# Probabilities times context in three rounded terms for four of twelve tiles

## The reference

```python
kv = context @ Wkv;  k, v = split(kv);  q = layernorm(x) @ Wq
dots = einsum('bhnd,bhmd->bhnm', q, k) * SCALE
dots = dots - (1 - mask)[:, None, :, None] * 1e6
out = einsum('bhnm,bhmd->bhnd', softmax(dots), v)
x = x + out @ Wout + bout
h = gelu(einsum('etd,edf->etf', layernorm(x).reshape(8, 56, 128), w1) + b1)
x = x + einsum('etf,efd->etd', h, w2) + b2
```

## Time and profile before

| what | us |
|---|---|
| median of 3 runs | 395.54 (395.53 to 396.33) |
| the profiled execution's own time | 395.39 |
| its span | 393.7 |
| a batch without a pair (155.94 to 195.70) | 39.76 |
| a batch with a pair (195.70 to 243.00) | 47.30 |
| DVE busy in these two | 30.19 and 36.49 |
| ACT busy in these two | 22.73 and 24.91 |

### The profile page before, as it was taken

The page is one execution under the profiler, slowest core; times in us unless marked ns, Lnnn a source line. Parts: engine busy times, 40 slices in busy tenths (PEclk is TensorE's granted clock), DMA queues, the critical chain, the costliest instruction groups (busy, mean ns, idle before and its releaser), DMA issues.

```text
span 393.7 us, 5563 instructions
## 1 busy us (share of the span) xinstructions
PE 384.8 (98%) x1701; PEld 277.6 (70%) x1701; DVE 282.7 (72%) x469; ACT 205.2 (52%) x273; POOL 63.7 (16%) x68
## 2 busy tenths in 40 slices
PE   7999999999999999999999999999999999999995
PEld 6667667767676777767776877667776776677674
DVE  4887778677867689677867688678867687266443
ACT  3546454565447444675356354575367344755421
POOL 0803401600070002500160003400250000000000
PEclk9999999999999999999999999999999999999999
DMA  7692010350035002142035003151121001200000
GB/s 246 208 273 51 10 69 1 92 144 0 2 83 152 2 1 63 44 149 93 3 91 140 0 0 78 39 169 60 33 73 49 0 0 31 82 2 0 3 2 3
DMA packets 23686, 25.00 MB, mean 64 GB/s; under 512 B 1240, under 2 KB 20600, under 8 KB 23672
## 3 DMA queue, kind: packets, MB, share of 16 engines
q1 hardware_dynamic: 20648, 19.45, 15.9%
q0 software_dynamic: 3024, 5.38, 5.3%
HBM read 24.59 MB, written 0.23 MB: 63 GB/s over the span
## 4 chain that ended last, share of the span: by engine, by line
PE 93%; DVE 4%; ACT 1%; DMA 1%; issue 1%; SPq 0%; DVEq 0%; ACTq 0%
PE ps_a L427 37%; PE ps_s L399 30%; PE ps_x L435 10%; PE ps_x L454 5%; PE ps_x L442 3%; PE ps_a L374 2%; PE ps_x L474 2%; PE ps_s L413 2%; PE ps_x L483 1%; DMA ex<-in_wk_t 1%; PE ps_x L413 1%; PE ps_x L347 1%; DVE chunk_max L765 0%; PE ps_s L367 0%; PE ps_a L347 0%
## 5 line engine op out<-in xcount | busy, mean ns | idle before, releaser
L427 PE MATMUL ps_a<-ex,ctx_sb 125*128 125x448 f32 x384 | 171.4, 541 | 0.0
L606 ACT ACTIVATE ex<-ps_s 125x896 f32<-125x896 f32 x96 | 88.1, 918 | 113.0 <-PE ps_s L399 82.1
L765 DVE TENSOR_REDUCE chunk_max<-ps_x 128x1 f32<-128x500 f32 x168 | 110.8, 674 | 42.2 <-PE ps_x L435 40.4
L427 PEld LDWEIGHTS ps_a<-ex,ctx_sb 125*128 125x128 f32 x384 | 71.3, 189 | 29.8 <-issue 23.9
L762 DVE TENSOR_TENSOR ex_sum<-ex_sum,ex 125x896 f32<-125x896 f32 x80 | 86.6, 1082 | 5.9 <-ACT ex L606 4.6
L435 PE MATMUL ps_x<-ctxt_hi,qk_hi 128*128 128x500 f32 x168 | 87.6, 524 | 1.0 <-DVE chunk_max L765 0.7
L399 PE MATMUL ps_s<-qk_hi,ctxt_hi 128*125 128x448 f32 x192 | 87.1, 534 | 0.0
L613 ACT COPY ps_s<-shift_row 125x896 f32<-125x896 f32 x80 | 72.9, 911 | 5.3 <-DVE shift_row L890 3.3
L399 PEld LDWEIGHTS ps_s<-qk_hi,ctxt_hi 128*125 128x125 f32 x192 | 35.9, 187 | 35.1 <-issue 35.0
L399 PE MATMUL ps_s<-qk_hi,ctxt_lo 128*125 128x448 f32 x192 | 57.3, 380 | 0.0
L399 PE MATMUL ps_s<-qk_lo,ctxt_hi 128*125 128x448 f32 x192 | 54.8, 367 | 0.0
(11 more groups left out here) (81 smaller groups left out, 256.0 us busy)
## 6 DMA issues: line engine op xcount, KB each, us to landing
ctxt_raw<-in_ctx_t SPq DMA_DIRECT2D x8, 750.0 KB, 8.6
ctx_sb<-in_ctx SPq DMA_DIRECT2D x8, 750.0 KB
ctxt_hi<-in_ctx_t POOLq DMA_DIRECT2D x21, 250.0 KB, 3.4
w_sb<-in_w SPq DMA_DIRECT2D x4, 512.0 KB, 3.8
w_sb<-in_w SPq DMA_DIRECT2D x8, 256.0 KB, 4.5
ex<-in_wq_t SPq DMA_DIRECT2D x2, 256.0 KB, 3.8
ex<-in_wk_t SPq DMA_DIRECT2D x2, 256.0 KB, 4.6
att_n<-in_wv_t SPq DMA_DIRECT2D x1, 512.0 KB, 6.1
```

The costliest lines, as they stand in the source:

```text
L427: mm = nc.tensor.matmul(ps_a[:, c, 0:CH], ctx_sb[0:MT, u, t, :], ex[0:MT, t % RING, c * CH:(c + 1) * CH], start=(t == 0), stop=(t == TM - 1))
L606: nc.scalar.activation(half(ex[0:MT, slot, :]), src, ACT.Exp, scale=SCALE).then_inc(ex_ready, 1)
L765: nc.vector.tensor_reduce(chunk_max[:, k, t:t + 1], filled()[:, 0:MC], AX.X, ALU.max).then_inc(job_free, 1)
```

## The change

For tiles 4, 6, 8 and 10 of each batch, `probs_ctx` is computed in three rounded float32r terms, as the scores are. ScalarE copies the exponentials into `ex_hi` and, once a batch, the four context tiles into `ctx_hi`; VectorE subtracts to make `ex_lo`, GpSimd to make `ctx_lo`. There is one buffer of each.

```diff
+    SPLIT = [4, 6, 8, 10]
+    CTX_HI_AT, CTX_LO_AT = 2, 5
...
+        def split_before(b, t):
+            n = SPLIT.index(t)
+            return b.at(TM, SPLIT[n - 1] + 1 if n else SPLIT[-1] + 1 - TM)
...
+                if t in SPLIT:
+                    n = SPLIT.index(t)
+                    if n == 0:
+                        pe.wait_ge(ctx_lo_ready, b.at(1, 1))
+                    pe.wait_ge(ex_lo_ready, b.at(len(SPLIT), n + 1))
+                    for term, (a, e) in enumerate([(ctx_hi, ex_hi), (ctx_hi, ex_lo), (ctx_lo, ex_hi)]):
+                        if term == 2 and between is not None:
+                            between()
+                        for c in range(2):
+                            mm = nc.tensor.matmul(ps_a[:, c, 0:CH], a[0:MT, n, :], e[0:MT, c * CH:(c + 1) * CH], start=False, stop=False)
+                    mm.then_inc(pv_done, 1)
+                    return
...
+            def ex_high_part(b, t):
+                act.wait_ge(ex_ready, b.at(TM, t + 1))
+                wait(act, pv_done, split_before(b, t))
+                nc.scalar.copy(ex_hi[0:MT, :], ex[0:MT, t % RING, :]).then_inc(ex_hi_ready, 1)
+
+            def ctx_high_part(b):
+                act.wait_ge(ctx_in[b.parity], b.at_every_other(16, 16))
+                wait(act, pv_done, split_before(b, SPLIT[0]))
+                nc.scalar.copy(ctx_hi[0:MT, :, :], split_tiles(b)).then_inc(ctx_hi_ready, 1)
...
                     if t + 2 < TM:
                         seed(b, t + 2)
+                    if t == CTX_HI_AT:
+                        ctx_high_part(b)
+                    if t in SPLIT:
+                        ex_high_part(b, t)
...
+            def ex_low_part(b, t):
+                dve.wait_ge(ex_hi_ready, b.at(len(SPLIT), SPLIT.index(t) + 1))
+                nc.vector.tensor_tensor(ex_lo[0:MT, :], ex[0:MT, t % RING, :], ex_hi[0:MT, :].bitcast(F32),
+                                        ALU.subtract).then_inc(ex_lo_ready, 1)
...
                     drain((t, 2))
                     between((t, 3))
+                    if t - 1 in SPLIT:
+                        ex_low_part(b, t - 1)
...
+            def ctx_low_part(b):
+                pool.wait_ge(ctx_hi_ready, b.at(1, 1))
+                nc.gpsimd.tensor_tensor(ctx_lo[0:MT, :, :], split_tiles(b), ctx_hi[0:MT, :, :].bitcast(F32),
+                                        ALU.subtract).then_inc(ctx_lo_ready, 1)
...
                 for t in range(TM):
+                    if t == CTX_LO_AT:
+                        ctx_low_part(b)
```

## The result

| | before | after |
|---|---|---|
| median, lowest and highest of 4 runs each, us | 395.53 (395.48 to 396.33) | 401.32 (399.51 to 402.35) |
| ratio, 95% interval | | 1.0137 [1.0091, 1.0182] |
| the profiled execution, its span | 395.39, 393.7 | 402.26, 400.4 |

What follows compares the result with a forecast made beforehand. PE, busy 98% of the span, was taken as the bound. Gains and waits summed to −0.75 (batch 0), 0 (batches 1, 3, 5), +4.95 (2, 4, 6) and +0.58 (7): +4.8 on 395.39, so 400.1 us, range 395.2 to 402.6.

Steps and rivals of the forecast that it cites:

- item 3: Job banks, pair batches: low parts of tiles 4 and 6 delay DVE's maxima, so PE's jobs wait; 0.4 us in all.
- PE's gain, 0.28 a tile: Split tiles: six rounded matmuls at 1.23 us replace four records at 1.51; 1.12 a batch, 9.0 us for 32 tiles.
- the rival at 0.54: DVE's low part: subtraction takes 0.54 us in the queue, not 1.00, giving 394.0 us; chance 0.10.
- Item 1: Tile 4, batches 1, 3, 5: low part comes behind DVE's sum and maximum, so PE waits 0.61 us.
- the door: Steps 3 to 5, batches 1 to 6: GpSimd's moved chunks hold DVE's `refine_inverse` at a shared SBUF door, 0.5 us each.
- Item 2: Tile 4, pair batches and batch 7: low part stands behind `residual` on DVE, so PE's product waits 0.40 us.
- Item 4: Tile 8, pair batches: low part stands where DVE's sum of step 10 began; product waits 0.37 us, batch 0 the same.
- Item 5: `out_job`: ACT's copy for tile 10 holds up the sigmoid and `gelu`; PE waits 1.1 us in pair batches, 0.5 in batch 7.
- The rival that `out_job`'s chain is covered: Pair batches and batch 7: `gelu_sigmoid` is not held, 3.8 us less, 396.3 us; chance 0.06.
- Item 6: Tile 10, batch 7: low part stands behind `output` on DVE, so PE's product waits 0.8 us.
- More collisions: Six batches: each `drain_sum` held too, or job banks at their upper bound, giving 402 to 408 us; chance 0.10.
- The door is no matter: Batches 1 to 6: GpSimd doesn't hold DVE's `refine_inverse`, without the six times 0.5, giving 397.1 us; chance 0.22.

Runs made afterwards that it cites:

- e0: Kernel after, with GpSimd's first subtraction in the prologue waiting for all three VectorE casts, not the first; 400.05 us, ratio 1.0096.
- e4: e0 without VectorE's subtraction for `ex_lo`, `ex_hi` taken in its place in the second term; 392.93 us (one run).
- e8: e0 with e1's and e2's edits (`ctx_lo` early in batch 0), some low parts moved earlier, `gelu` and cap before the sum over tiles; 388.09 us, ratio 0.9774.
- e2: e0 with GpSimd's context subtraction moved behind both `ctxt_lo` chunks; 398.88 us, ratio 1.006.
- e5: e0 with all parts made and waited for, but the product multiplied in plain float32; 407.56 us (one run).
- e1: e0 with ScalarE's copy of tile 10 behind the two sigmoid functions in pair batches and batch 7; 397.59 us, ratio 1.0022.
- e3: e0 with all products plain, keeping only the context parts and PE's wait for them, their result unused; 396.92 us, ratio 1.0019.
- e11: e8 with tile 2 split as well, its low part early in step 3; 390.33 us, ratio 0.9865.

## Why the prediction was right, point by point

The forecast case came true: 401.32 against 400.1, with its mechanisms in their places but for one part of item 3. The batches gave +3.9, not +4.8, and the start-up of the profiled execution put 2.8 on top, which no step of mine foresaw; without it this execution would lie near 399.5, and e0, with the same batches, is at 400.05. So the closeness of 400.1 to the median is in part luck: the batches were forecast 0.9 too slow, and two of the four runs, the profiled one among them, are some 2 us slower than the other two.

- *PE's gain, 0.28 a tile.* Right: −1.10 a batch in e4, and e8's pieces are 0.81 (3 tiles), 1.05 (4) and 1.37 (5) under those of before. In the queue of batch 3 the six matmuls take 1.22.
- *The subtraction at 1.08, the rival at 0.54.* The subtraction is 1083 ns in all 32: the rival that ended faster is out.
- *The ACT copy.* Taken as 0.9, it is 0.94; the prediction's 0.85 in a full queue fits (154.62 to 155.47).
- *Item 1 with the door, 0.61 + 0.5.* Measured 0.93 for both (−0.19 + 1.12). e2 takes off 0.32 and leaves 39.74, that is 0.61 of wait: item 1 was exact, the door was mis-sized. I ended GpSimd's second chunk 0.5 behind `refine_inverse`'s start; it was 0.49, and the instruction was held 0.35 of it, since it ran 0.14 ahead of the end of GpSimd's record. The same 0.14 stands in my own working for the other order, and I didn't use it here. Six times 0.15 is 0.9, nearly all of the distance between +4.8 and +3.9.
- *Item 2, 0.40:* 0.41 in batch 2, 0.43 in batch 7. *Item 4, 0.37:* 0.31; batch 0 has 0.41 in all.
- *Item 3, 0.4:* 0.14 + 0.26, right in size and by luck. The 0.26 is not the low parts' doing, as e4 and e5 show: it is tile 6's gain, which a chain from `hidden_job` on takes back.
- *Item 5, 1.1, in batch 7 0.5:* 1.19 (1.12 of it idle) and 0.50. Right as a sum; as a mechanism it was half of the story. I costed one chain, through ACT, and e1 shows a second one 0.5 to 0.6 shorter, through DVE's queue. The rival that `out_job`'s chain is covered had 3.8 us for it; ordering ACT alone gives 3 × 0.63 + 0.46.
- *Item 6, 0.8:* 0.71. Tile 8 of batch 7 has no wait, as I had it.
- *More collisions:* out. `drain_sum` isn't held, and the banks cost 0.40, not their upper bound. The bounds named for the forecast's own range add up to 398.0 and 402.8, not to its 398.4 and 402.0.
- *The door is no matter (the rival at 397.1):* refuted by e2 and e3 together. The Trainium skill, SBUF — State Buffer, section "Who interferes with whom", says that a VectorE instruction with two SBUF inputs contends with a GpSimd instruction that reads SBUF, and that one with at most one SBUF input, outside the two-port modes, does not. This case's traces agree: `refine_inverse` 1.09 to 1.44, e11's low part 1.08 to 2.14, while the two `drain_sum` from 173.57 on run beside GpSimd's chunks with one input in PSUM and aren't held: all sixteen take 0.61 to 0.63 (mean 0.62 before).

The half of the answer that the prediction didn't look for is that nearly all of its waits were questions of order. By the page DVE had 79% and so seemed the limit that the four tiles ran into; e8 does the same work with the same engines and gains 7.9 of the 9.0 us. The wait of 0.26 in step 9 of a pair batch is left, and that is a chain, not DVE's load. Where the amount of work on DVE becomes the limit is not shown: e11's fifth tile loses, but its low part is also held by GpSimd, and no run has the one without the other.

## What to carry to other kernels

Where work is added to in-order queues, cost each new instruction at every place where it may stand, not only where it was put: here the order alone was worth 12 us of 400 (e0 against e8), and a second buffer no more than one swap. When one wait is removed, look what else was late by the same time; the next layer was half of the first. Time saved on an engine is not gained where a chain from that engine's own earlier work sets the pace: from `hidden_job` to step 10 it stays 7.3 us with tile 6's product at 1.51 or 1.23. And judge a variant by the lengths of its repeated parts when its start-up varies by more than the effect.

## What the runs showed of the hardware

- A VectorE instruction held by GpSimd doesn't show as idle before it but as its own duration: 1.44 instead of 1.09, and 2.14 instead of 1.08. GpSimd is held the same way: `ctx_lo` took 1.80 beside DVE's sum, and 1.28 where it came first (batch 0 of e2).
- The start-up, nearly the same instructions in all of these kernels, varied by up to 3.3 us in the profiles (batch 0 began at 30.9 to 34.3), with the granted clock at 0.83 in a window where another execution had 1.00. In the kernel after, 1.6 of its 2.8 us lie in the stretch at 0.50 to 0.51. None of the twelve experiments explains why the clock fell there.
